# Message stage of a graph network kernel: the last message product and the carry copies move behind a group's third product on VectorE

## The reference

```python
h = 2.0 ** 0.5 * relu(emb @ W1 / 10.0 ** 0.5)                 # 16 values an edge
w = (h @ W2 / 16.0 ** 0.5).reshape(E, 7, 16, 8)               # per edge, seven 16 x 8 weights
s_out, g_out = sums over u of features of both ends * w[...]   # 8 scalars and 8 gates
v_out = sums over u of features, direction * w[...]            # 8 vectors of 3
s_act, gates = 1.593 * tanh(s_out), 1.593 * tanh(g_out)
edge_ftr = concatenate([s_act, gates[:, :, None] * v_out]) * norm[:, None]
x = layernorm(x + segment_sum(edge_ftr, dst))
```

## Time and profile before

| | |
|---|---|
| median of 3 runs | 4437.76 us (4434.99 to 4440.44) |
| the profiled execution | 4443.45 us |
| its span in the trace | 4441.7 us |
| granted TensorE clock, mean over the span | 0.953 |
| VectorE in the message stage | first product of line 900 at 373.5 us, last at 2523.6 us |

### The profile page before, as it was taken

How to read it: one execution, slowest core, us unless ns; L and a number is a source line. 1 busy time by engine, 2 the same in 40 slices (tenths; PEclk the granted TensorE clock), 3 DMA queues, 4 the chain that set the end, 5 groups by cost and what they waited for, 6 DMA issues and landing times. The chain is left out here.

```text
span 4441.7 us, 66461 instructions
## 1 busy us (share of the span) xinstructions
PE 3333.9 (75%) x20487; PEld 2105.1 (47%) x20487; DVE 3024.5 (68%) x4871; ACT 2187.2 (49%) x4787; POOL 3235.5 (73%) x3260
## 2 busy tenths in 40 slices
PE   0005888888888888888888604999999999999940
PEld 0002333333333333323323203999999999999940
DVE  5525999999999999999999733344444544444432
ACT  3004555555555555555555311466666666666620
POOL 5777777777777777777774077777777777777756
PEclk9999999999999999999999856999999999999975
DMA  9311222222222222222222102133333333333311
GB/s 325 90 49 34 49 48 48 55 50 47 48 48 48 48 50 53 48 47 48 48 47 43 34 12 68 42 72 73 72 73 72 73 72 73 72 73 72 73 29 27
DMA packets 269592, 272.69 MB, mean 61 GB/s; under 512 B 182593, under 2 KB 237673, under 8 KB 266803
## 3 DMA queue, kind: packets, MB, share of 16 engines
q1 hardware_dynamic: 164150, 207.75, 17.0%
q0 software_dynamic: 104928, 60.74, 9.6%
q10 hardware_dynamic: 462, 3.60, 0.3%
HBM read 181.82 MB, written 90.02 MB: 61 GB/s over the span
## 5 line engine op out<-in xcount | busy, mean ns | idle before, releaser
L640 POOL DMA_INDIRECT edge<-xp_d,idx x1440 | 1447.3, 1005 | 439.1 <-issue 425.1
L900 DVE TENSOR_TENSOR prod<-G_ps,hid 128x1000 f32<-128x1000 f32 x1200 | 1400.4, 1195 | 125.8 <-PE G_ps L782 113.1
L1297 POOL DMA_INDIRECT x1e<-tab_d,idxb x1122 | 1105.4, 985 | 342.7 <-issue 336.4
L782 PE MATMUL G_ps<-FT,wst 32*128 32x500 f32 x4800 | 896.3, 633 | 356.8 <-DVE prod L900 350.0
L1346 PE MATMUL G_ps<-tb,hot 128*126 128x442 f32 (+1 forms) x3968 | 799.1, 358 | 0.9 <-DVE x1e L1371 0.8
L1346 PEld LDWEIGHTS G_ps<-tb,hot 128*126 128x126 f32 x3968 | 742.7, 187 | 38.4 <-DVE x1e L1371 2.0
L782 PEld LDWEIGHTS G_ps<-FT,wst 32*128 32x128 f32 x4800 | 246.3, 184 | 792.2 <-DVE prod L900 724.6
L811 PE MATMUL R_ps<-prod,red 128*32 128x500 f32 x4800 | 589.7, 594 | 0.0
L702 ACT ACTIVATE hid<-T_ps 128x500 f32<-128x500 f32 x400 | 233.8, 585 | 677.4 <-PE T_ps L802 677.1
L1346 PE MATMUL T_ps<-tb,hot 128*126 128x442 f32 x2000 | 416.4, 360 | 186.3 <-DVE one_d L1430 186.3
L1346 PEld LDWEIGHTS T_ps<-tb,hot 128*126 128x126 f32 x2000 | 376.6, 188 | 205.0 <-issue 186.4
(11 more groups left out here) (240 smaller groups left out, 4290.1 us busy)
## 6 DMA issues: line engine op xcount, KB each, us to landing
xd_d<-zeros SPq DMA_DIRECT2D x16, 1562.5 KB, 29.2
y_d<-ng SPq DMA_DIRECT2D x40, 595.0 KB
edge<-xp_d,idx POOLq DMA_INDIRECT x1440
xv<-xd_d SPq DMA_DIRECT2D x40, 560.0 KB
y_d<-zr SPq DMA_DIRECT2D x40, 560.0 KB
x1e<-tab_d,idxb POOLq DMA_INDIRECT x1122
edge<-sel_d SPq DMA_DIRECT2D x20, 750.0 KB
edge<-sel_d SPq DMA_DIRECT2D x20, 687.5 KB
```

The source lines that it names most:

```text
L640: nc.gpsimd.indirect_dma_start(out=edge_c[:, i, 8:8 + DIM], out_offset=None, in_=xp_d, in_offset=bass.IndirectOffsetOnAxis(col, 0)).then_i ...
L782: return Tn.matmul(G_ps[pair][:, a * 512:a * 512 + GW], wst[rows, r * 128:(r + 1) * 128], FT[k][rows, :], start=True, stop=True)
L900: V.tensor_tensor(prod[b][i][:, :].rearrange("p (a e) -> p a e", a=2), gv, hid[k][:, :].rearrange("p (a e) -> p a e", a=1).broadcast_to([1 ...
L1297: nc.gpsimd.indirect_dma_start(out=gx[b][:, c * T1:(c + 1) * T1], out_offset=None, in_=tab_d, in_offset=bass.IndirectOffsetOnAxis(idx[b][: ...
```

## The change

`post(2)`, the last message product, goes from the odd group (between second and third product) to the end of the even group in which steps 0 and 1 of the same piece stand, behind the scan. `carry_sums` goes behind the third product of group 4, behind the message steps 0 and 1 and in front of the last message product. `carry_x` goes from group 0 to the end of group 9 of the chunk before, and one call for the first is added in front of the first turn. The products, scans, sizes and all other engines' programs are the same.

```diff
                             multiply(n, k, b, 0)
                             multiply(n, k, b, 1)
-                            if k == 1 and not (first and g < 5):
-                                q = (g - 5) // 2
-                                post(2, t * RING + q, q % RING // PC, q % RING % PC, t if q >= 0 else t - 1)
-                            if gc == 0 and not (last and h == 1):
-                                carry_x(ch + 1, 1 - h)
-                            if gc == 4 and not (first and h == 0):
-                                carry_sums(ch - 1, 1 - h, t - 1 + h)
                             multiply(n, k, b, 2)
                             if k == 1:
                                 q = (g + 5) // 2
@@ -972,12 +965,20 @@
                                     scan()
                                 if more:
                                     along(t * RING + q, q % RING)
-                            elif not (first and g < 4):
+                                if gc == GC - 1 and not last:
+                                    carry_x(ch + 2, h)
+                            else:
                                 q = (g - 4) // 2
-                                for i in range(2):
-                                    post(i, t * RING + q, q % RING // PC, q % RING % PC, t if q >= 0 else t - 1)
-                            if k == 0 and scan:
-                                scan()
+                                due = not (first and g < 4)
+                                if due:
+                                    for i in range(2):
+                                        post(i, t * RING + q, q % RING // PC, q % RING % PC, t if q >= 0 else t - 1)
+                                if scan:
+                                    scan()
+                                if gc == 4 and not (first and h == 0):
+                                    carry_sums(ch - 1, 1 - h, t - 1 + h)
+                                if due:
+                                    post(2, t * RING + q, q % RING // PC, q % RING % PC, t if q >= 0 else t - 1)
@@ -991,6 +992,7 @@
                     for p in range(3):
                         turned(p, p, 0, 0, 0)
                         along(p, p)
+                    carry_x(1, 1)
                     turn(0, first=True)
```

## The result

The changed kernel takes 4414.44 us in the median of 5 runs (4413.76 to 4419.40), the kernel before, beside it, 4440.44 (4434.99 to 4443.48): 26.0 us less, a ratio of 0.9946 with a 95% interval of 0.9931 to 0.996. The forecast was 28.7 us less, 4409.1, in a range of 4403 to 4425. Of the 5.3 us between forecast and result, 2.7 are a smaller gain, and 2.7 are the kernel before, which measured 4440.44 here and not 4437.76.

A forecast was written before the change was run, and what follows sets the result against it. In the message stage TensorE paces even groups and VectorE paces most odd ones. 198 odd groups gaining 0.145 us give 28.7, all other terms cost 0: 4437.76 - 28.7 = 4409.1 us, range 4403 to 4425.

The forecast's parts named there:

- the band of the forecast: Whole kernel: the forecast as made keeps a chance of 0.74, between 4404 and 4413 us.
- rival A: Even scan groups: cover a little short, 160 groups grow by 0.06 us, 10 us given back, 4419; chance 0.14.
- Part 1: Odd groups: without the last message product the third product starts 0.145 us earlier, 198 groups, 28.7 us gained.
- Part 2: End of the even group: the moved product fits under TensorE's chain, 0.02 us of cover left, cost 0.
- Rival B: End of the even group runs at full length, 37 to 50 us paid, about 4452 us; chance 0.06.
- Parts 3 and 4: Carry of the sums later in group 4, carry of the column to group 9's end: both fit idle time, cost 0.
- Rival C: Something else holds the odd group's third product, or POOL becomes the pace: no gain, about 4438 us; chance 0.06.

The follow-up runs named there:

- e8: Changed kernel with TensorE's second sum round moved from the even group to the odd one, in front of round 2: 4383.72 us against 4436.24 for the kernel before.
- e4: Changed kernel without the last message product in the turns, tiles `O` zeroed ahead of the stage: 4411.79 us against 4434.12 for the kernel before.
- e3: Changed kernel with the last message product in the odd group, behind the third product: 4465.21 us against 4434.12 for the kernel before.
- e1: Changed kernel with both carries back in their old places: 4408.35 us against 4434.12 for the kernel before.
- e10: Changed kernel, unaltered, measured again beside e9: 4411.89 us against 4437.98 for the kernel before.
- e7: Changed kernel with ten already met waits in front of VectorE's loop: 4412.0 us in one run.
- e2: Changed kernel with the last message product back between second and third product of the odd group, only the carries moved: 4436.15 us against 4434.12 before.
- e5: Changed kernel with the last message product in front of the scan instead of behind it: 4420.22 us against 4436.24 for the kernel before.
- e6: Changed kernel with a second product of the same size behind the moved one, into a spare tile: 4456.89 us against 4436.24 for the kernel before.
- e9: Kernel of e8 with the last message product back between second and third product of the odd group: 4355.78 us against 4437.98 for the kernel before.

## Why the prediction was right

**The time.** 4414.44 lies in the range, but 1.4 us above the band of the forecast (4404 to 4413) and inside the one that the prediction gives to rival A. By the gain, 26.0 us off 4437.76, it would be 4411.8. The time alone doesn't tell the two apart; the lengths of the groups do, and they speak for the forecast's path.

**What paces the groups**, TensorE the even ones and VectorE the odd ones, held and is shown: e8 shortens TensorE's chain and group 4 follows by 0.52; e4 takes VectorE's instruction away and the even group does not follow; e3 puts it into the odd group, which follows by its full 0.33.

**Part 1**, 0.145 us in each of 198 odd groups: the third product starts at +2.41 as put. In the traces the gain is 0.142 in most scan groups and 0.15 in those without one. It is 0.11 in group 5 of each half, where the first scan of the sums takes 0.86 instead of 0.83 us. Together it is 26.7 us instead of 28.7. With 0.11 in 40 of the groups and nearly 0.145 in the others, group 5 makes 1.4 of the missing 2.0. That scan is as long in e1 and e4 (0.86) and e10 (0.85), takes 0.84 in e7, and 0.83 in e2, e3, e5, e6, e8 and e9. So neither the carries' new places nor the last message product itself, which e4 does not have, is needed for it; what lengthens it is open.

**Part 2**, cost nothing at the end of the even group, by a hair: right, in all even groups but one. That nothing is paid e4 shows (taken away, no gain). The spare cover, 0.02 us in the prediction, is 0.03 to 0.04 by the runs: in e6 0.36 more work cost 0.33, in e5 0.12 cost 0.09, and where VectorE paces in e8 an even scan group takes 5.39, 0.04 less than with TensorE's chain. What the step did not see is group 12, 2.0 us in all: rival A in small, but for another reason than the overlap of neighbours. From the moved product to the next first product it is 0.31 to 0.32 in e8, where TensorE does not set that start, and 0.35 to 0.36 in the changed kernel, where it does; rival A had put 0.42. e5 shows that "behind the scan" was needed and not only "in the even group".

**Rival B** did not occur: no group end ran at full length. By the rule of the Trainium skill that the prediction cites ("VectorE: DVE Perf Modes", "The DRAIN you can't avoid"), each instruction would start behind the end of the one before. The prediction left out that section's last sentence, by which a next op that is not held starts earlier. The rows here fit that sentence and not the bare rule: without a wait a start comes before the end of the instruction before (0.34 us behind a start for a span of 0.50), and behind it where the instruction waits for its direct predecessor's result (e5, 0.03 behind the end).

**Parts 3 and 4**, the carries at nothing: right, by e2 (1.0, 0.999 to 1.0009), but for the lateness of group 12, which e1 without them does not have.

**Rival C**, POOL: did not occur, though one of its numbers was off. I had POOL's turn fixed at 104.7 us; it is 103.6 in the changed kernel (1440 gathers from 512.8 to 2376.8). So POOL still gains 2.5 us a turn on VectorE's 106.13, about as before, and not the 1.2 of the prediction.

**The sum** was 28.7; the stage gave 24.8 from its first to its last group in the trace, and the medians 26.0. The terms that were mis-sized are the gain of group 5 (1.4 us too much) and the cost of group 12 (2.0 us, put at 0); the other 0.6 is 0.004 us in each of the other odd groups.

## What to carry to other kernels

When two engines hand work back and forth, write down for each kind of step which engine's chain ends last, and count an instruction's cost in start-to-start distances: the same instruction cost 0.33 us in a step paced by its own engine, about 0.14 where it partly filled a wait, and nothing in a step paced by the other engine. Such an order is right only for the pace it was found with. When the other engine's chain is shortened, look again at everything that was moved under it: here undoing the move then brought about 28 us more.

## What the runs showed that was not expected

- Some 160 instructions into VectorE's loop one comes 0.1 us late in every turn, a semaphore instruction in the kernel before and a product in the changed one. It matters only where no slack covers it, and ten waits already met ahead of the loop made it harmless (e7).
- POOL's rate follows VectorE's. Its gathers take 0.95 us, but some in each turn take 1.05 to 1.5, and their excess differs from kernel to kernel: 80 gathers took 104.7 us before, 103.6 in the changed kernel, 104.8 in e8 and 103.3 through most of e9. In the last two that is the length of VectorE's turn to 0.1 us, while the trace names no wait of either engine for the other. The traces do show where the long gathers lie: in the kernel before, the changed one and e8, each gather of the loop over 1.0 us (246, 212 and 262 of 1440) overlaps a scan of VectorE, and none of those that overlap no scan is that long. So how many of them are lengthened depends on how the two loops lie to each other. In e5, e6 and e9 32 to 36 long ones lie over another VectorE instruction instead. What lengthens a gather there was not tried. In e8 POOL's lead over VectorE stays the same from the loop's first turn on; in e9 it does for ten turns and then shrinks by 5 us, so a still shorter turn may meet it.
